# Masks of the first cross attention's turned scores by blocks of 32 queries, and the recurrence's tokens loaded in two parts

## The reference, cut to what matters

```python
def _lstm(x, W_ih, W_hh, b_ih, b_hh):
    xg = jnp.einsum('bsd,gd->bsg', x, W_ih) + b_ih + b_hh
    def step(carry, xg_t):
        h, c = carry
        g = xg_t + h @ W_hh.T
        i, f, gg, o = jnp.split(g, 4, axis=-1)
        c = jax.nn.sigmoid(f) * c + jax.nn.sigmoid(i) * jnp.tanh(gg)
        h = jax.nn.sigmoid(o) * jnp.tanh(c)
        return ((h, c), h)
    _, hs = lax.scan(step, init, xg.transpose(1, 0, 2))
...
def _L0_xattn_ref(q, k, v, Wq, bq, Wk, bk, Wv, bv, Wo, bo, mask):
    ...
    scores = jnp.einsum('bhqd,bhkd->bhqk', qh, kh) / jnp.sqrt(jnp.float32(dk))
    scores = jnp.where(mask[:, None, :, :] == 0, jnp.float32(NEG), scores)
    attn = jax.nn.softmax(scores, axis=-1)
    ctx = jnp.einsum('bhqk,bhkd->bhqd', attn, vh)
    ...
x = _layernorm(x + _L0_attn_ref(x, ...))
x = _layernorm(x + _L0_xattn_ref(x, ctx_1024, ctx_1024, ..., mask_BxSxS2_ik1))
```

## Time and profile before

| | us |
|---|---|
| median of three runs | 1857.99 |
| the profiled execution's own time | 1860.04 |
| its span | 1858.1 |
| PE busy | 1526.8 (82%) |
| DVE busy | 1110.8 (60%) |
| ACT busy | 874.0 (47%) |
| POOL busy | 610.4 (33%) |

### The profile page before, as it was taken

The page is one execution under the profiler, slowest core; times in us unless marked ns, Lnnn a source line. Parts: engine busy times, 40 slices in busy tenths (PEclk is TensorE's granted clock), DMA queues, the critical chain, the costliest instruction groups (busy, mean ns, idle before and its releaser), DMA issues.

```text
span 1858.1 us, 43723 instructions
## 1 busy us (share of the span) xinstructions
PE 1526.8 (82%) x16300; PEld 1015.0 (55%) x16300; DVE 1110.8 (60%) x3614; ACT 874.0 (47%) x2556; POOL 610.4 (33%) x849
## 2 busy tenths in 40 slices
PE   4555369988989778898889833699799999998998
PEld 3334246645656465555557512477577777776443
DVE  3434445555766656314767688577566666664776
ACT  2222334454546444344546544344366666665443
POOL 1422231122226433101212233222244444443666
PEclk6555569999999888899999955599899999999999
DMA  6000000000000000000020000000000000000000
GB/s 237 2 1 2 1 1 2 2 1 2 2 2 2 2 0 1 1 1 2 2 118 2 10 15 1 1 3 3 24 1 1 0 0 0 0 0 1 1 12 12
DMA packets 5144, 21.84 MB, mean 12 GB/s; under 512 B 2665, under 2 KB 2921, under 8 KB 3561
## 3 DMA queue, kind: packets, MB, share of 16 engines
q1 hardware_dynamic: 4970, 19.49, 2.8%
HBM read 18.15 MB, written 1.05 MB: 10 GB/s over the span
## 4 chain that ended last, share of the span: by engine, by line
PE 66%; DVE 12%; issue 7%; ACT 6%; POOL 4%; DVEq 3%; POOLq 1%; DMA 0%; ACTq 0%; SPq 0%
PE ps L726 5%; PE ps L650 5%; PE ps L689 5%; PE ps L2854 4%; PE ps L2503 4%; PE ps L2513 3%; PE ps L2527 3%; PE ps L2482 3%; PE ps L2489 3%; PE ps L2326 2%; PE ps L1289 2%; PE ps L610 2%; PE ps L736 2%; PE ps L2474 2%; PE ps L713 2%
## 5 line engine op out<-in xcount | busy, mean ns | idle before, releaser
L913 DVE TENSOR_REDUCE arena<-ps 128x4 f32<-128x512 f32 x320 | 204.4, 684 | 124.6 <-PE ps L675 41.7
L851 ACT ACTIVATE arena<-ps 128x512 f32<-128x512 f32 x320 | 171.7, 597 | 113.1 <-PE ps L713 110.7
L541 POOL TENSOR_TENSOR arena<-arena,C 128x512 f32<-128x512 f32 x80 | 83.1, 1040 | 405.0 <-ACT arena L872 139.6
L2419 POOL TENSOR_TENSOR arena<-arena 128x512 f32<-128x512 f32 x128 | 132.6, 1042 | 224.5 <-DVE arena L2728 224.0
L1289 PE MATMUL ps<-hid,WA 128*20 128x16 f32 x1024 | 57.1, 196 | 87.7 <-DVE hid L1340 87.7
L2646 ACT COPY arena<-ps 128x512 f32<-128x512 f32 x128 | 69.1, 588 | 123.2 <-PE ps L2513 123.2
L2637 ACT ACTIVATE arena<-ps,arena 128x256 f32<-128x256 f32 x256 | 119.9, 477 | 11.8 <-issue 8.1
L2854 PE MATMUL ps<-WA,maskadd 128*128 128x512 f32 x256 | 119.8, 598 | 1.8 <-DVE arena L2997 1.8
L726 PE MATMUL ps<-arena 128*32 128x128 f32 x2560 | 110.9, 282 | 3.2 <-ACT arena L851 3.0
L650 PE MATMUL ps<-arena 32*128 32x128 f32 x2560 | 103.8, 288 | 10.1 <-POOL arena L541 7.0
L2720 DVE TENSOR_REDUCE arena<-ps 128x2 f32<-128x512 f32 x128 | 82.5, 686 | 45.0 <-PE ps L2503 43.6
(11 more groups left out here) (455 smaller groups left out, 3841.8 us busy)
## 6 DMA issues: line engine op xcount, KB each, us to landing
WA<-w_late SPq DMA_DIRECT2D x1, 4228.0 KB, 13.4
WA<-w_early SPq DMA_DIRECT2D x1, 1600.0 KB
R<-rows SPq DMA_DIRECT2D x1, 1282.0 KB, 6.7
WB<-w_rest SPq DMA_DIRECT2D x1, 1152.0 KB, 9.8
xT_all<-x_T SPq DMA_DIRECT2D x1, 1024.0 KB, 6.4
x_all<-x_tok SPq DMA_DIRECT2D x1, 1024.0 KB, 11.8
arena<-mask SPq DMA_DIRECT2D x1, 1024.0 KB
ctxT_all<-ctx_T SPq DMA_DIRECT2D x1, 1024.0 KB
```

Source lines behind the costliest of these rows:

```text
L541: nc.gpsimd.tensor_tensor(heads(v_(n % 2, ATT, "P", WIDE_Q, 512)), src.unsqueeze(1).broadcast_to([128, 4, 128]), cst("tilemask").unsqueeze ...
L851: nc.scalar.activation(v_(s, ATT, "PT", 512 * t, 512), ps[s][t][:, :], ACT.Exp, scale=SCALE).then_inc(pT_sb, 1)
L913: nc.vector.tensor_reduce(v_(z, ATT, "m", 4 * t, 4), heads(ps[z][t][:, :]), AXX, ALU.max)
L2419: nc.gpsimd.tensor_tensor(p, p, v_(z, LAT, "rec", 4 * u + 2 * x, 2).unsqueeze(2).broadcast_to([128, 2, 256]), ALU.mult).then_inc(l_sub, 1)
```

## The change

The turned mask of X0 takes the form that MQA has. POOL signals `mask_made` when all 16 masks are there. SP then copies them with 32 DMAs into `mask_4`, in two places of `arena` that are free at the time: for each group t and block b, the 32 queries of block b for sequences 0 to 11, and for 12 to 15. In `scores_T` the four products of 128 rows by 512 columns become 16 products of 32 rows by 128 columns. The mask of `scores` (L675) stays.

The tokens are stored with time outermost (`xT_tok`), the host's array likewise. The first 16 tokens are loaded right after the first weights. The other 112 tokens and the constants follow the recurrence's bias rows. The four casts of constants move from the start of DVE's program to behind step 4 of the recurrence, where DVE waits for the constants and the other tokens, and PE waits for these before the inputs at step 8.

```diff
@@ scores_T
                 elif mask_kind is not None:
-                    for t in T_ORDER:
-                        nc.tensor.matmul(heads(ps[s][t][:, :]), maskadd[:, n, :],
-                                         ident_b[:, :].unsqueeze(1).broadcast_to([128, 4, 128]), start=False,
-                                         stop=False, skip_group_check=True)
+                    if n == 0:
+                        pe.wait_ge(masks_in, 512)
+                    for b in range(4):
+                        for t in T_ORDER:
+                            nc.tensor.matmul(heads(ps[s][t][:, :])[:, :, 32 * b:32 * b + 32], mask_4_of(n)[rows(t), b, :],
+                                             ident_b[rows(t), rows(t)].unsqueeze(1).broadcast_to([32, 4, 32]),
+                                             start=False, stop=False, skip_group_check=True)
@@ loads
+        mask_4 = [arena[s][:, QKV_KEPT:QKV_KEPT + 256 * n].bitcast(BF16).rearrange("p (n b k) -> p n b k", n=n, b=4)
+                  for s, n in enumerate((12, 4))]
             sp.dma_start(WA[:, 0:164], w_early[:, 0:164]).then_inc(first_in, 16)
-            sp.dma_start(C[:, :], const).then_inc(first_in, 16)
-            sp.dma_start(xT_all[:, :, :], x_T).then_inc(first_in, 16)
+            sp.dma_start(xT_tok[:, 0:STEPS, :], x_T[:, 0:STEPS, :]).then_inc(first_in, 16)
...
                 sp.dma_start(bias3[k:k + 1, 0:LSTM_BIAS], bias_parts[0:LSTM_ROWS, k, :]).then_inc(bias_rows, 16)
+            sp.dma_start(xT_tok[:, STEPS:TOK, :], x_T[:, STEPS:TOK, :]).then_inc(const_in, 16)
+            sp.dma_start(C[:, :], const).then_inc(const_in, 16)
...
+            sp.wait_ge(mask_made, 1)
+            for t in range(4):
+                for b in range(4):
+                    to, of = slice(32 * t, 32 * t + 32), slice(32 * b, 32 * b + 32)
+                    sp.dma_start(mask_4[0][to, :, b, :], maskadd[of, 0:12, :]).then_inc(masks_in, 16)
+                    sp.dma_start(mask_4[1][to, :, b, :], maskadd[of, 12:16, :]).then_inc(masks_in, 16)
@@ start_dve, and const_dve new
-            nc.vector.tensor_copy(ident_b[:, :], ident)
-            ... (three more casts)
+        def const_dve(dve):
+            dve.wait_ge(const_in, 32)
+            nc.vector.tensor_copy(ident_b[:, :], ident)
+            ... (the same three)
@@ lstm_pe, inputs
-                xs = xT_all[:, :, bass.ds(it * STEPS + half * HALF, HALF)].rearrange("p b t -> p t b")
+                xs = xT_tok[:, at:at + HALF, :]
@@ lstm_pe, lstm_dve
+                    if g == HALF:
+                        pe.wait_ge(const_in, 32)
...
+                if g == CONST_AT:
+                    const_dve(dve)
```

More of the change, by code:

```diff
@@ L192, in decoder @@
         late_in = sem("late_in")
+        const_in = sem("const_in")
         rest_in = sem("rest_in")
@@ L199, in decoder @@
         fours_in = sem("fours_in")
+        mask_made = sem("mask_made")
+        masks_in = sem("masks_in")
         bias_cut = sem("bias_cut")
@@ L1004, in name_cols, with mask_4_of @@
             return c(name, of, width)
+        STEPS, HALF = 16, 8
+        xT_tok = xT_all[:, :, :].rearrange("p b t -> p (b t)").rearrange("p (t b) -> p t b", b=BATCH)
+        mask_4 = [arena[s][:, QKV_KEPT:QKV_KEPT + 256 * n].bitcast(BF16).rearrange("p (n b k) -> p n b k", n=n, b=4)
+                  for s, n in enumerate((12, 4))]
+        def mask_4_of(n):
+            return mask_4[n // 12][:, n % 12, :, :]
         def loads(sp):
@@ L1037, in loads @@
                     sp.dma_start(ident_4[to, b, :], ident_b[of, :]).then_inc(fours_in, 16)
-        loads_first, loads_early, loads_rest = 3, 4, 7
+            sp.wait_ge(mask_made, 1)
[4 more added lines that the diff above has]
+                    sp.dma_start(mask_4[1][to, :, b, :], maskadd[of, 12:16, :]).then_inc(masks_in, 16)
+        loads_first, loads_early, loads_rest = 2, 4, 7
         LSTM_BIAS = LSTM_ROWS * BIAS_COLS
@@ L1087, in start_dve @@
             dve.wait_ge(first_in, 16 * loads_first)
-            nc.vector.tensor_copy(ident_b[:, :], ident)
-            nc.vector.tensor_copy(causal_b[:, :], cst("causal"))
-            nc.vector.tensor_copy(pick_b[:, :, :], cst("foldmask").unsqueeze(2).broadcast_to([128, 4, 128]))
-            nc.vector.tensor_copy(negrow_b[:, :], cst("second").broadcast_to([128, REG_ROWS])).then_inc(const_cast, 1)
             ih, hh, ms = W_of("ih"), W_of("hh"), W_of("musig")
@@ L1099, in start_dve @@
             dve.sem_inc(const_b, 1)
+        def const_dve(dve):
+            dve.wait_ge(const_in, 32)
+            nc.vector.tensor_copy(ident_b[:, :], ident)
+            nc.vector.tensor_copy(causal_b[:, :], cst("causal"))
+            nc.vector.tensor_copy(pick_b[:, :, :], cst("foldmask").unsqueeze(2).broadcast_to([128, 4, 128]))
+            nc.vector.tensor_copy(negrow_b[:, :], cst("second").broadcast_to([128, REG_ROWS])).then_inc(const_cast, 1)
         def mean_dve(dve, n):
@@ L1155, in start_pool @@
             pool.drain()
+            pool.sem_inc(mask_made, 1)
             for b in range(BATCH):
@@ L1199, in start_pool @@
             pool.sem_inc(seq_done, 2)
-        STEPS, HALF = 16, 8
+        CONST_AT = 4
         gate_banks = [ps[0][1], ps[0][2]]
@@ L1267, in inputs @@
             def inputs(it, half, gt):
-                xs = xT_all[:, :, bass.ds(it * STEPS + half * HALF, HALF)].rearrange("p b t -> p t b")
+                at = it * STEPS + half * HALF
+                xs = xT_tok[:, at:at + HALF, :]
                 o = bank(half % 2, gt)
@@ L3333 @@
     arrays = {
-        "x_tok": a["x"].transpose(1, 0, 2), "x_T": a["x"].transpose(2, 0, 1),
+        "x_tok": a["x"].transpose(1, 0, 2), "x_T": a["x"].transpose(2, 1, 0),
         "ctx_tok": a["ctx_1024"].transpose(1, 0, 2), "ctx_T": a["ctx_1024"].transpose(2, 0, 1),
```

## The result

The changed kernel takes 1840.89 us (median of 4 runs, 1840.31 to 1842.72) against 1857.8 for the one before (four runs, the three above and one more): ratio 0.9909, 95% interval 0.9894 to 0.9924. The profiled execution took 1842.72, 17.3 us less than the one shown of before.

What follows compares the result with a forecast made beforehand. The recurrence was taken as a chain of short steps, X0 as bound by PE. From 1860.04 us, -13.6 - 2.5 + 0.1 + 0.6 = -15.4 gave 1844.6 profiled, 1842.6 median; 8-in-10 range 1838.5 to 1847.

Steps and rivals of the forecast that it cites:

- Masks, -13.6: X0's turned mask products: 0.85 us less for each of 16 sequences, 13.6 us in all, read from MQA's same operation.
- The waits behind the masks: PE's waits in X0 after the masks come 0.85 us earlier but all stay ahead, so nothing is lost.
- The slack of L948: In X0, DVE's read of a bank ahead of the next scores: slack 1.30 us before, 0.45 after.
- Start, -2.5: Kernel start: PE begins at 7.3 instead of 9.84 us, released by the bias rows; gain 2.5, between 1.9 and 2.9.
- the landing of the third bias row: At the start, the last bias row, issued at about 5.1, lands between 6.8 and 7.8 us, taken as 7.2.
- Casts, +0.1: Four casts of constants moved into the recurrence, mostly covered by DVE's idle 0.70 us a step: cost 0.1 us, once.
- Mask copies: 32 DMAs between POOL's last mask and X0's first turned masks: at most 152 us of issue, hidden, costed at nothing.
- the slower rival: Mask copies issued at 42 ns a piece, ready at 399 us; X0 waits 135 us, time 1978; chance 0.04.
- Clock at X0's start: Clock's rise at X0's start may not move with PE's earlier work: loss between nothing and 1.25 us, taken as 0.6.
- The rest: Later stages: no term in the sum, about 2 us either way as half-clock stretches may fall differently.

Runs made afterwards that it cites:

- changed_again: The changed kernel itself measured once more, unaltered, beside kernels with further additions on the same chip: 1841.14 us, ratio 0.9908.
- both_by_rows: Against the changed kernel, the mask of X0's other scores also by sixteen products of 32 rows: 1838.38 us, ratio 0.9893.
- combined_first: Changed kernel plus both X0 masks by 32 rows (first sequence's scores masked as before), one bias row issued by ACT, POOL's memset later: 1835.12 us, ratio 0.9879.

## Why the prediction was right

The forecast was 1842.6 us for a median and 1844.6 for a profiled execution; 1840.9 and 1842.7 came. Term by term:

- Masks, -13.6: right. 0.86 us a sequence for 0.85, and X0 as a whole 13.8 shorter. The nearest row was the same operation in MQA. The packed products take 0.22 us; the 3.07 times of the Trainium skill ("TensorE: Matmul & The Clock Gate", section "Why this matters for your kernels") would have put them at 0.32. That X0 as a whole gave just 16 x 0.86 is partly luck: the clock rose equally late in the two profiled executions, 9.4 us behind the first scores. In the six other profiles of kernels with this X0 and the new casts X0 shortened by 15.5 to 15.9.
- The waits behind the masks, nothing: right. The slack of L948 was 0.43 for 0.45 forecast, and the products' removal showed that 0.22 less was hidden too.
- Start, -2.5: the largest miss, 3.1 came. The mis-sized term is the landing of the third bias row: I took 7.2 between 6.8 and 7.8, and it was 6.7. The row's least value (1.7 us from the start of the issue) was the right one, since nothing large was in the queue. Its median of 2.7 came from copies in a crowd: those issued at 24 us, with the DMA engines busy 0.99 of the time, took 9.1 us to land, those issued from 39 us on 1.7 to 2.2. What I said ends the wait, the bias rows, was right: they release PE at 6.73. What I had not read is that before the change DVE's way ended in the same moment (9.87 for 9.84); the change shortened both, so the sum did not suffer.
- Casts, +0.1: 0.0. The other tokens landed at 10.4 and the constants at 12.4, ahead of the 13 forecast.
- Mask copies, nothing: right. An issue of 384 pieces took 0.61 us, as one of 32 does; the slower rival rested on a price by the piece that does not exist there. The 0.59 that I set against it were not all "alone": the first of those copies were issued from 24 to 30 us, with the DMA engines 0.99 busy, so busy engines did not lengthen these issues.
- Clock at X0's start, +0.6: 0.0 in this execution. The rise moved with the work (to 264.3 us from 267.4; granted 0.69 in 252 to 272 us, and 0.61 before), and in changed_again it came earlier still (259.7, granted 0.81). I had not bounded it below nothing, and it can be a gain of 2 us; that this execution showed none is chance. Nor had I read right what went ahead of it: PE was busy without a pause from 262.55, not from 264.8.
- The rest, nothing: -0.4 here: a little over 0.1 each in the recurrence with the positional attention, behind X0, and outside the span.

The differences, 0.6 for the start, 0.1 for the casts, 0.6 for the clock, 0.2 for the masks and 0.4 for the rest, make up the 1.9 us between the forecast and the profiled execution.

## What to carry to other kernels

Where a kernel holds the same operation in another form elsewhere, the distance between the rows on either side of it is the price to use, with what the array loses between 32 and 128 rows included: it was 0.25 us for each way there and back here, as much as a short group of products. A tiny transfer that everyone waits for belongs ahead of the large ones, but only bytes that are still in the queue when its turn comes count; and before a wait is taken away, see whether a second one ends at the same moment, as at 9.84 and 9.87 here. And when a product is cut into blocks, look at the first round of the pipeline too, where what was finished bank by bank now ends all at once.

## What the runs showed that I had not expected

- DVE's scalings of 128 by 60 floats took 0.97 to 1.19 us while POOL's memset ran, 0.19 without it; a subtraction of 128 by 16 took 1.03 in place of 0.18 while POOL multiplied (L933 of both_by_rows).
- An issue by ACT's queue took 1.28 us for what SP issues in some 0.7 to 0.9, yet side by side they gained 0.7 us.
- The clock's rise at X0's start differs between executions of one kernel. From the first L692 to the fold it took 2.3 us in the profiled execution of the changed kernel and 1.2 in changed_again, and by X0's end they stood 1.85 us apart. A difference of two single profiles can hold some 2 us of this.
- The recorded clock can be wrong: both_by_rows and combined_first have a granted clock of 1.00 in 205 to 250 us, but their first 32 score products at 254 to 255 us took 2.09 us, as in the kernel before at 0.50, and 1.11 at full clock.
